# Attention stage: the loop over pairs of chunks written as straight code on all five engines

## The reference, cut to what matters

```
h   = mamba_output                       # 32 x 512 tokens, 256 wide
x1  = layernorm(layernorm(h))            # scales worked out together
q, k, v = split(x1 @ qkv.T)              # 16 query heads, 4 key heads of 16
a   = softmax(causal(q k^T) / 4) v       # over the 32 entries of one position
hh  = first_input + a @ proj.T
x2  = layernorm(hh)
p   = softmax(x2 @ router); top 2 of 8   # and where each row goes
```

## Time and profile before

| what | value |
|---|---|
| median of 3 runs | 4695.05 us (4687.83 to 4703.43) |
| the profiled execution's own time | 4694.2 us |
| its span, first to last instruction | 4692.6 us |
| PE busy | 4084.0 us, 87% |
| DVE busy | 3868.6 us, 82% |
| ACT busy | 2676.8 us, 57% |
| POOL busy | 2214.4 us, 47% |
| granted TensorE clock, mean | 0.864 |

### The profile page before, as it was taken

How to read it: one execution, slowest core, us unless ns; L and a number is a source line. 1 busy time by engine, 2 the same in 40 slices (tenths; PEclk the granted TensorE clock), 3 DMA queues, 4 the chain that set the end, 5 groups by cost and what they waited for, 6 DMA issues and landing times. The chain is left out here.

```text
span 4692.6 us, 75960 instructions
## 1 busy us (share of the span) xinstructions
PE 4084.0 (87%) x20868; PEld 3138.8 (67%) x20869; DVE 3868.6 (82%) x7673; ACT 2676.8 (57%) x4136; POOL 2214.4 (47%) x1865
## 2 busy tenths in 40 slices
PE   5989998999999999999997888888888189888988
PEld 3666666666666666666665676767666189888988
DVE  6999999999999999999997666666667277777777
ACT  4666676666666667666765555555555043434343
POOL 2444444434343434343435355555555445555555
PEclk7888888888888888888888888887888599999999
DMA  2111010111010101111111122222222345445554
GB/s 59 30 27 35 26 35 26 35 26 38 24 37 24 38 28 32 30 30 30 30 30 38 62 74 83 77 78 76 84 84 76 105 76 92 82 89 87 85 87 75
DMA packets 181894, 255.69 MB, mean 54 GB/s; under 512 B 22881, under 2 KB 126690, under 8 KB 181858
## 3 DMA queue, kind: packets, MB, share of 16 engines
q1 hardware_dynamic: 120930, 157.20, 11.7%
q0 software_dynamic: 60928, 98.09, 10.9%
HBM read 138.63 MB, written 116.59 MB: 54 GB/s over the span
## 5 line engine op out<-in xcount | busy, mean ns | idle before, releaser
L539 PE MATMUL pj<-xt,win 128*128 128x512 f32 x3144 | 982.5, 469 | 51.6 <-DVE xt L708 37.2
L539 PEld LDWEIGHTS pj<-xt,win 128*128 128x128 f32 x3144 | 685.0, 221 | 281.1 <-issue 85.3
L294 POOL TENSOR_TENSOR wk<-v,uc 128x512 f32<-128x512 f32 x260 | 334.3, 1286 | 694.1 <-DVE v L770 693.6
L1942 POOL DMA_INDIRECT out<-e_y,e_to x272 | 445.4, 1637 | 426.4 <-DVE e_y L2089 355.2
L587 PE MATMUL po<-yz,wout 128*128 128x512 f32 x1024 | 484.5, 629 | 72.2 <-DVE h1o L857 44.8
L721 DVE SCALAR_TENSOR_TENSOR uc<-pj,convw,uc 128x511 f32<-128x511 f32 (+2 forms) x780 | 518.4, 730 | 13.5 <-ACT uc L360 13.5
L1992 PE MATMUL e_p<-e_w,e_a 128*128 128x256 f32 x3264 | 421.5, 287 | 43.1 <-DVE e_a L2082 43.1
L1980 PE MATMUL e_p<-e_xt,e_w 128*128 128x256 f32 x3264 | 411.5, 283 | 39.0 <-DVE e_xt L2070 38.0
L1992 PEld LDWEIGHTS e_p<-e_w,e_a 128*128 128x128 f32 x3264 | 401.9, 195 | 44.7 <-DVE e_a L2082 44.7
L1980 PEld LDWEIGHTS e_p<-e_xt,e_w 128*128 128x128 f32 x3264 | 392.0, 189 | 48.0 <-issue 47.3
L587 PEld LDWEIGHTS po<-yz,wout 128*128 128x128 f32 x1024 | 199.2, 200 | 310.0 <-issue 309.1
(11 more groups left out here) (247 smaller groups left out, 9292.0 us busy)
## 6 DMA issues: line engine op xcount, KB each, us to landing
e_x<-expert_in SPq DMA_DIRECT2D x137, 260.0 KB
bb<-bc SPq DMA_DIRECT2D x65, 512.0 KB, 4.8
a_h<-h_rows SPq DMA_DIRECT2D x136, 128.0 KB
h_rows<-h1o SPq DMA_DIRECT2D x32, 512.0 KB, 5.5
a_hb<-h_rows SPq DMA_DIRECT2D x128, 128.0 KB
out<-a_bs SPq DMA_DIRECT2D x128, 128.0 KB
bc<-xd SPq DMA_DIRECT2D x65, 128.0 KB, 2.2
e_w1s<-in_moe_w POOLq DMA_DIRECT2D x10, 512.0 KB
```

Of the source, the lines that this page charges most:

```text
L294: pool.tensor_tensor(wk[:, m, :], v[:, m, :], uc[d][:, m, :], ALU.mult).then_inc(S["dtu_ok"], 1)
L539: i = mm(pj[m][:], win[d][wp][:, k, c:c + P], xt[xp][:, k, :], start=(k == 0 and n == 0), stop=(k == KD - 1 and n == 2))
L1942: pool.indirect_dma_start(out=out, out_offset=bass.IndirectOffsetOnAxis(ap=to[n][:, j:j + 1].bitcast(U32), axis=0), in_=y[n][:, j, :], in_ ...
```

## The change

In all five engines' programs the hardware loop becomes a Python loop, so that the 30 slots are written out one behind the other, and c is an integer in each. In the loader of SP the test whether c is an integer goes, since it always is one now.

```
             def load(dst, c, name):
-                b0 = c * BB if isinstance(c, int) else (c * BB) % SEQ
+                b0 = (c * BB) % SEQ
                 for j in range(TT):
@@ on sp, pool, act, pe and dve alike @@
             slot(0, 0)
             slot(1, 1)
-            with pe.Fori(1, NCH // 2) as h:
+            for h in range(1, NCH // 2):
                 slot(2 * h, 0)
                 slot(2 * h + 1, 1)
```

More of the change, by code:

```diff
@@ L1067, in _ @@
             slot(1)
-            with sp.Fori(1, NCH // 2) as h:
+            for h in range(1, NCH // 2):
                 slot(2 * h)
@@ L1184, in _ @@
             slot(1, 1)
-            with pool.Fori(1, NCH // 2) as h:
+            for h in range(1, NCH // 2):
                 slot(2 * h, 0)
@@ L1288, in _ @@
             slot(1)
-            with act.Fori(1, NCH // 2) as h:
+            for h in range(1, NCH // 2):
                 slot(2 * h)
@@ L1639, in _ @@
             slot(1, 1)
-            with dve.Fori(1, NCH // 2) as h:
+            for h in range(1, NCH // 2):
                 slot(2 * h, 0)
```

## The result

The changed kernel takes 4646.5 us (median of 4 runs, 4630.9 to 4666.8) beside 4699.2 for the kernel before (4 runs): ratio 0.9891, 95% interval 0.9855 to 0.9927, 53 us less. Run again beside the kernel before in e9, the ratio was 0.9869 [0.9848, 0.9890]. The prediction of 4690 us was wrong, and 4646 lies outside its range.

The account below looks back on a forecast made before the run. PE was taken to set the pace in attention, slowed by a stall in each slot from the third on. The profiled 4694.2 us less 2.6 and 1.4 gave 4690 us; 8-in-10 range 4655 to 4722 us.

Parts of the forecast that it names:

- The issues of SP: SP's four load DMAs per slot: issued in 2.25 us instead of 2.86, 0.61 us less, taken as 0 gain.
- Waking from a wait: DVE's value worked out before L1514, for whose sum PE waits 13 times: -1.4 us, bounds 0 and -2.9.
- the common stall: Stretch in each slot from the third on, when scatter and load run together and PE and DVE mostly stand.
- the stall falls better: Rival on looped slots: earlier DVE and SP bring one in six from 35.5 to 30.9 us; -21 us, 4669; chance 0.30.
- PE isn't moved: Argument against the better-stall rival: scatter and load move together in the slot, while PE does not; no size given.
- The clock: PE's granted clock, 0.84 over the 27 slots, expected to stay near that; lower after PE has stood still.
- The branches: 15 loop turns on each engine lose register add, compare and branch: taken as 0, bounds 0 and 3 us.
- fetches: Instruction fetch for the longer code, some 37 more PE packets: taken as 0, bounds 0 and +38 us.
- DVE's register instructions: On DVE's chain to `a_core`, 0.33 us less a slot, counted 8 times: -2.6 us, bounds 0 and -9.
- PE no longer waits for `a_core`: PE's 3.5 us of waits, in 8 gaps, for DVE's normalised chunk should nearly vanish.

Follow-up runs that it names:

- e9: The changed kernel itself (all five engines straight), run again beside the kernel before: 4639.4 us, ratio 0.9869.
- e1: The kernel before with only DVE's loop written as straight code, the other four looped: 4697.7 us, ratio 0.9988.
- e3: The kernel before with only SP's loop written as straight code: 4698.3 us, ratio 0.9981.
- e11: The kernel before with all loops but PE's written as straight code, on a chip with the stall: 4645.8 us, ratio 0.9874.
- e10: The kernel before with only PE's loop written as straight code, on a chip with the stall: 4699.2 us, ratio 0.9992.
- e5: The kernel before with only PE's loop written as straight code, where the kernel before took 4602.6 us: 4613.9 us, ratio 1.0014.
- e12: The changed kernel with SP's load held back until the scatter has landed, on a chip with the stall: 4616.5 us, ratio 0.9817 of the kernel before.
- e7: The changed kernel with SP's load held back until the scatter has landed, without the stall: 4572.4 us, ratio 0.9955 of the kernel before.
- e8: The kernel before, all engines looped, with SP's load held back until the scatter has landed, without the stall: 4585.6 us, ratio 0.9940.
- e16: The kernel before, all engines looped, with SP's load held back until the scatter has landed, run again without the stall: 4587.2 us, ratio 0.9967.

## Why the prediction was wrong

*The step that failed* is the one that took a stall for a fixed thing: in "The issues of SP", that the load "lies in it just the same", and in "Waking from a wait", that most of the wait for `a_hh` "is the common stall" and stays, with 1.4 us off. Measured, the wait fell by 32.4 us, the waits before the scores by 25.7 more, and 25.0 came back before L1331. What was missing is that the order of events around the stall can change: in the changed kernel the second sum is on time, ahead of the stretch in which DVE stands, in 22 (e9: 24) of 27 slots, before in 10, and PE then has its scores done when its instructions begin to come 0.7 us apart. Which instruction less, on which engine, brings the sums ahead of the stall stays open.

*The rival "the stall falls better"* named the right kind of case with its sign, but its size was wrong: one slot in six from 35.5 to 30.9 us, -21 us. What came is a mean that fell from 33.13 to 30.90 over all 27 slots. Its ground, DVE 0.33 and SP 0.6 us earlier, fell too: e1 and e3 have one each and gain nothing that can be told. "PE isn't moved" was no argument against it, since e11 has the whole gain with PE looped.

*The clock* was not in the sum. It was read in the earlier trace rows and used for the rival alone, yet PE's shorter busy time carries 32.7 of the 60.2 us.

*What was right.* The branches and fetches together cost and gave nothing that can be told: 38 more packets on q8 for 37 predicted, 36 more on q14 for 35, and e10, with all of PE's 38, is at 0.9992. In the 27 slots they are

```profile
q8 instruction: 37, 0.61, 0.3%
q14 instruction: 37, 0.30, 0.1%
```

and e5, which drops PE's 15 taken branches and adds its 38 packets where there is no stall, is at 1.0014: by the lower end of its interval, 0.9989, the branches gave back at most 5 us, 0.3 us each, unless the fetches cost as much as they gave. The Trainium skill, "Runtime: NRT & Kernel Launch", section "Instruction fetch mechanics", would have such branches stall for a fetch; for this loop these runs show no such stall, and the earlier trace rows no such fetch. DVE's register instructions: L1579 to L1607 takes 1.18 or 1.19 us in 18 of the 27 slots, as predicted, and up to 1.49 in the others; L1574 to L1468 takes 0.26 us in most, for 0.21 predicted; SP's four issues take 2.30 us for 2.25; and PE no longer waits for `a_core`:

```profile
2947.85 0.18 DVE L1579 TENSOR_TENSOR a_row<-a_pb,a_seen 128x32 f32<-128x32 f32 x1
...
2949.03 0.16 DVE L1607 TENSOR_TENSOR a_xs<-a_first,a_xs 128x4 f32<-128x4 f32 x1
```

*Settled, and not.* Shown: the gain belongs to the stall around the scatter. It is there, twice, where the kernel before takes 4700 us, and seven runs of five kernels that between them hold every part of it show nothing beyond 0.2%, none of it outside the error, where it takes 4600 (the changed kernel itself wasn't run there). Neither DVE, SP nor PE carries it alone, and PE isn't needed. Not shown: whether ScalarE's or GpSimd's straight code is what counts or a combination, since those runs met no stall; why PE's instructions come 0.7 us apart in it and DVE stands; and why three of five groups don't have it. Each group had a chip of its own, and within one the executions of the kernel before agree (4683 to 4730 us in the first, 4585 to 4629 in the second), so the chip and whatever else differed between the groups can't be told apart. That every register instruction costs a like delay in the stall fits the order of the table's ends but not its middle (e1 and e3), and in the slot of before four of DVE's sequencer instructions run from 2851.92 to 2852.19, 0.1 us apart, once DVE goes on; it stays a guess.

## What to carry to other kernels

When an idle time has the releaser "issue" or "remote", don't hold it fixed in a sum: list what is due just before and in it, and bound the change by all of those turning up in time (here 34 + 36 us of waits, and the clock with them). Price the clock with the idle time: here 27.5 us less of PE's idle time went with 32.7 us less for the same matmuls. And before reading a few tenths of a per cent, see that the kernel before takes its usual time beside it: an experiment on a stall tells nothing where the stall is not.

The fastest kernel of this case is e12, straight code with the load held back until the scatter has landed: 4616.5 us, all 4 runs (4613.0 to 4620.5) below the 4 of the changed kernel beside it (4631.5 to 4643.6), and 0.9817 of the kernel before. In e7, e8 and e16 the later load gave 0.9955, 0.9940 and 0.9967 without a stall.

## What was not expected of the hardware

- The same program takes 4700 us in two groups of runs (and in the runs shown first) and 4600 in three, each group on a chip of its own, nearly all of it in the looped slots: 33.1 us a slot before, and 29.2 to 29.5 in kernels with parts of the change.
- While GpSimd's indirect DMAs run, PE's instructions can come one each 0.7 us instead of one each 0.12 us (32 scores in 3.77 us), and DVE stands up to 7 us, often until 1.8 to 2.0 us after the last of them has ended; ACT too starts late, 1.3 us in e12's slot and 2.0 in the slot of the changed kernel above. GpSimd itself keeps its pace, one indirect DMA each 1.27 us with the stall and without.
- The DMA queues move 160 to 172 GB/s in both cases, so the rate doesn't tell whether a stall is on.
